# Retention block with a mixture-of-experts layer: router logits as extra columns of the V and output projections, ranking on raw logits

## What is computed

```
x = x + retention(layernorm(x)) @ Wo
x = x + experts(layernorm(x))
```

```
logits = einsum('btd,de->bte', x, Wg)
probs = softmax(logits); top_w, top_i = top_k(probs, 2)
top_w = top_w / (sum(top_w) + 1e-08)
h = square(relu(einsum('td,edh->teh', xt, W1)))
y = einsum('teh,ehd->ted', h, W2)
out = einsum('te,ted->td', combine, y)
```

## Time and profile before

| | |
|---|---|
| median of 3 runs | 290.26 us (289.76 to 290.81) |
| profiled execution, its own time | 288.95 us |
| profiled execution, span | 287.2 us |
| TensorE busy | 274.8 us (96%) |
| weight loads of TensorE | 216.4 us (75%) |
| VectorE busy | 222.4 us (77%) |
| ScalarE busy | 179.3 us (62%) |
| GpSimd busy | 206.1 us (72%) |
| granted TensorE clock, mean | 0.998 |
| 16 DMA engines, main queue | 28.5% of their span |

### The profile page before, as it was taken

How to read it: one execution, slowest core, us unless ns; L and a number is a source line. 1 busy time by engine, 2 the same in 40 slices (tenths; PEclk the granted TensorE clock), 3 DMA queues, 4 the chain that set the end, 5 groups by cost and what they waited for, 6 DMA issues and landing times.

```text
span 287.2 us, 8936 instructions
## 1 busy us (share of the span) xinstructions
PE 274.8 (96%) x3662; PEld 216.4 (75%) x3662; DVE 222.4 (77%) x569; ACT 179.3 (62%) x257; POOL 206.1 (72%) x165
## 2 busy tenths in 40 slices
PE   7999868899999999999999999999999999999995
PEld 5685547678887788777887788777887788878883
DVE  2759758995769875996869965896859768998783
ACT  2345476565782688555974677556875567586861
POOL 2115889879959697769968699569968668566452
PEclk9999999999999999999999999999999999999999
DMA  7329062222250261204440240103420252043101
GB/s 227 120 82 295 5 214 71 86 63 96 70 147 2 78 185 60 89 11 126 128 147 2 79 179 23 59 5 103 157 75 2 77 152 92 19 130 130 75 0 73
DMA packets 13577, 26.80 MB, mean 93 GB/s; under 512 B 1120, under 2 KB 6624, under 8 KB 13536
## 3 DMA queue, kind: packets, MB, share of 16 engines
q1 hardware_dynamic: 13536, 26.23, 28.5%
HBM read 24.00 MB, written 2.23 MB: 91 GB/s over the span
## 4 chain that ended last, share of the span: by engine, by line
PE 52%; POOL 21%; issue 16%; DVE 5%; DMA 2%; ACT 2%; POOLq 1%; DVEq 0%; ACTq 0%
POOL act_lo L1062 17%; PE h_ps L333 7%; PE y_ps L348 6%; PE h_ps L335 6%; PE h_ps L334 5%; PE y_ps L354 5%; PE y_ps L349 5%; PE bank L480 2%; PE bank L492 2%; PE bank L413 2%; POOL x_lo L1032 2%; POOL rstd L1016 1%; PE bank L445 1%; DMA scale<-scratch 1%; PE y_ps L312 1%
## 5 line engine op out<-in xcount | busy, mean ns | idle before, releaser
L1062 POOL TENSOR_TENSOR act_lo<-act_f,act_hi 128x512 fp32r<-128x512 f32 x112 | 145.9, 1325 | 47.7 <-ACT act_f L950 47.6
L760 DVE SCALAR_TENSOR_TENSOR act_s<-h_ps,scale 128x1024 f32<-128x1024 f32 x64 | 77.9, 1217 | 31.1 <-issue 13.6
L945 ACT ACTIVATE act_hi<-act_s 128x1024 fp32r<-128x1024 f32 x64 | 67.9, 1061 | 33.7 <-DVE act_s L760 33.1
L950 ACT ACTIVATE act_f<-act_s 128x1024 f32<-128x1024 f32 x64 | 67.0, 1046 | 0.0
L333 PE MATMUL h_ps<-x_hi,w_lo 128*128 128x512 f32 x128 | 54.1, 422 | 1.0 <-DVE attn L653 1.0
L348 PE MATMUL y_ps<-act_hi,w_lo 128*128 128x512 f32 x128 | 53.9, 421 | 0.0
L335 PE MATMUL h_ps<-x_hi,w_hi 128*128 128x512 f32 x128 | 50.5, 395 | 0.0
L334 PE MATMUL h_ps<-x_lo,w_hi 128*128 128x512 f32 x128 | 50.5, 394 | 0.0
L349 PE MATMUL y_ps<-act_hi,w_hi 128*128 128x512 f32 x128 | 50.3, 393 | 0.0
L354 PE MATMUL y_ps<-act_lo,w_hi 128*128 128x512 f32 x128 | 40.2, 395 | 0.1
L1016 POOL TENSOR_TENSOR rstd<-variance,minus_half 128x4 f32<-128x4 f32 x16 | 17.9, 1119 | 19.1 <-DVE variance L617 18.9
(11 more groups left out here) (121 smaller groups left out, 402.3 us busy)
## 6 DMA issues: line engine op xcount, KB each, us to landing
scale<-scratch SPq DMA_DIRECT2D x32, 512.0 KB, 4.0
x_t_in<-x_tr SPq DMA_DIRECT2D x8, 256.0 KB, 4.8
x_all<-x SPq DMA_DIRECT2D x8, 256.0 KB, 4.6
out<-out_sb SPq DMA_DIRECT2D x8, 256.0 KB, 4.1
scale<-w SPq DMA_DIRECT2D x1, 768.0 KB, 4.8
cst<-constants SPq DMA_DIRECT2D x1, 417.0 KB, 6.0
cst<-constants SPq DMA_DIRECT2D x1, 256.0 KB, 2.8
scale<-w SPq DMA_DIRECT2D x1, 256.0 KB, 6.7
```

The lines of the kernel that those rows point to most:

```text
L760: nc.vector.scalar_tensor_tensor(out=act_s[:, u % 2], in0=h_ps[:, u % 2], scalar=0.0, in1=scale[:, f % 2, e].unsqueeze(1).to_broadcast([P, ...
L945: nc.scalar.activation(act_hi[:, u % 4], act_s[:, u % 2], ACT.Square).then_inc(act_hi_ready, 1)
L950: nc.scalar.activation(act_f[:, u % 2], act_s[:, u % 2], ACT.Square).then_inc(act_f_ready, 1)
L1062: nc.gpsimd.tensor_tensor(act_lo[:, u % 4, n], act_f[:, u % 2, n], act_hi[:, u % 4, n].bitcast(F32), ALU.subtract).then_inc(pool_low_ready, 1)
```

## The change

Router logits are linear in x, so they are gathered where x is made. The table of constants is laid out anew: the centred weight of V carries the 8 router columns beside its 128 (`w_vg`), and the output weight carries `Wo @ Wg` (centred, made once by `route_outputs` and `copy_route`). `project_v` and `project_out` give 136 columns a group; the fourth group goes into another PSUM bank. ScalarE copies the 8 columns of V's result behind x in `x_all` (136 wide now), and `add_attention` adds the rest. `route` and its copy are gone. VectorE ranks the raw logits (`rank_experts`), shifts the ranked ones (`shift_logits`), sums (`weigh`) and marks the two chosen (`mark_chosen`). The root of a share is now the exponential of half the logit (`half_expd`) times the power -1/2 of the denominator (`root_denominators`), which VectorE multiplies in `spread_roots`. The order on every engine is changed with it.

```diff
         def v_place(s, g):
+            if g == GROUPS - 1:
+                return ((y_ps[:], h_bank[3])[s] if s < 2 else bank1[:])[:, 0:WIDE]
+            return ((bank1[:], h_bank[2])[s] if s < 2 else bank2[:])[:, WIDE * g:WIDE * (g + 1)]
...
             def project_v(s):
...
                 elif s >= 2:
                     pe.wait_ge(q_m_ready, s + 1)
                     pe.wait_ge(q_d_ready, s + 1)
+                    pe.wait_ge(x_hi_ready, s)
...
-            def route(s):
...
                 if p < TILES:
                     if n == 0:
                         project_out(p)
                     if n == 2:
                         transpose_x2(p)
-                    if n == 5:
-                        route(p)
...
                     if n == 1:
-                        project_qk(a)
+                        project_k(a)
                     if n == 3:
+                        project_q(a)
+                    if n == 4:
                         transpose_k(a)
-                    if n == 4:
+                    if n == 5:
                         project_v(a)
...
+            def rank_experts(s):
+                raw = x_all[:, s % X_RING, :, P:WIDE]
+                dve.wait_ge(x2_ready, s + 1)
+                for g in range(GROUPS):
+                    last = nc.vector.max(best[:, g], raw[:, g])
+                last.then_inc(rank_step, 1)
...
             def spread_roots(s):
-                dve.wait_ge(root_ready, s + 1)
-                dve.wait_ge(choose_step, CHOOSE_STEPS * (s + 1))
+                dve.wait_ge(r_denom_ready, s + 1)
+                dve.wait_ge(expd_ready, s + 1)
+                nc.vector.tensor_tensor(root[:], half_expd[:], r_denom[:].unsqueeze(2).to_broadcast([P, GROUPS, TOP]),
+                                        ALU.mult).then_inc(spread_step, 1)
...
                 if p < TILES:
                     add_attention(p)
                     statistics(p, 1)
-                if a < TILES:
-                    decay_q(a)
                 scale_h(f, 1)
                 low(u)
+                if p < TILES:
+                    rank_experts(p)
+                    shift_logits(p)
                 if a < TILES:
                     decay_k(a)
+                    decay_q(a)
                 scale_h(f, 2)
                 low(u + 1)
                 if p < TILES:
-                    shift_logits(p)
+                    weigh(p)
+                    mark_chosen(p)
                 scale_h(f, 3)
                 low(u + 2)
                 if p < TILES:
-                    choose(p)
+                    spread_roots(p)
                 if a < TILES:
                     decay_scores(a, decay_order(a)[0:1])
                 scale_h(f, 4)
                 low(u + 3)
                 if a < TILES:
-                    decay_scores(a, decay_order(a)[1:2])
-                if p < TILES:
-                    spread_roots(p)
-                if a < TILES:
-                    decay_scores(a, decay_order(a)[2:])
+                    decay_scores(a, decay_order(a)[1:])
...
                 for g in range(GROUPS):
+                    nc.scalar.copy(x_all[:, s % X_RING, g, P:WIDE], v_place(s, g)[:, P:WIDE])
...
             copy_roots(0)
+            copy_o(1)
+            copy_k(2)
             high_second()
-            copy_o(1)
-            mask_q(2)
-            copy_k(2)
             high_qk()
...
-            def root_shares(s):
-                pool.wait_ge(share_ready, s + 1)
+            def root_denominators(s):
+                pool.wait_ge(denom_ready, s + 1)
                 if s >= 1:
-                    pool.wait_ge(combine_ready, s)
+                    pool.wait_ge(spread_step, SPREAD_STEPS * (s - 1) + 1)
+                nc.gpsimd.tensor_tensor(r_denom[:], denom[:, 2], minus_half[:], ALU.pow).then_inc(r_denom_ready, 1)
```

More of the change, by code:

```diff
@@ L93, in build @@
         minus_half = sb("minus_half", [P, GROUPS])
-        half = sb("half", [P, GROUPS * TOP])
         stats = sb("stats", [P, 2, STAT_RING, GROUPS, 6])
@@ L412, in project_v @@
                 for g in range(GROUPS):
-                    last = pe.matmul(v_bank(s)[:, P * g:P * (g + 1)], x_t_in[:, s % XT_RING, P * g:P * (g + 1)],
-                                     w_center[:, 2], start=True, stop=True)
+                    last = pe.matmul(v_place(s, g), x_t_in[:, s % XT_RING, P * g:P * (g + 1)], w_vg, start=True, stop=True)
                 last.then_inc(v_done, 1)
@@ L498, in project_out @@
                 if s == 0:
-                    pe.wait_ge(second_loaded, DMA)
+                    pe.wait_ge(wog_ready, 1)
                 pe.wait_ge(o_t_ready, s + 1)
                 for g in range(GROUPS):
-                    last = pe.matmul(bank1[:, P * g:P * (g + 1)], o_t[:, s % 2, g], w_out, start=True, stop=True)
+                    last = pe.matmul(out_place(g), o_t[:, s % 2, g], w_out, start=True, stop=True)
                 last.then_inc(wo_done, 1)
@@ L507, in transpose_x2 @@
                 for g in range(GROUPS):
-                    last = pe.transpose(bank1[:, P * g:P * (g + 1)], x_all[:, s % X_RING, g], ident)
+                    last = pe.transpose(bank1[:, P * g:P * (g + 1)], x_all[:, s % X_RING, g, 0:P], ident)
                 last.then_inc(t2_done, 1)
-            def route(s):
-                pe.wait_ge(x_sum_ready, s + 1)
-                if s == 0:
-                    pe.wait_ge(piece_whole, 1)
-                else:
-                    pe.wait_ge(x_hi_ready, s + 1)
-                for g in range(GROUPS):
-                    last = pe.matmul(route_bank(s)[:, EXPERTS * g:EXPERTS * (g + 1)], x_sum[:, s % SUM_RING, P * g:P * (g + 1)],
-                                     wg_whole[:], start=True, stop=True)
-                last.then_inc(router_done, 1)
             def transpose_roots(s):
@@ L607, in statistics @@
                 for g in range(GROUPS):
-                    last = nc.vector.bn_stats(stats[:, which, r, g], xs[:, g])
+                    last = nc.vector.bn_stats(stats[:, which, r, g], xs[:, g, 0:P])
                 last.then_inc(norm_step[which], 1)
@@ L709, in choose, with weigh, weighed @@
+            def weigh(s):
+                def weighed(n):
+                    dve.wait_ge(weigh_step, WEIGH_STEPS * s + n)
                 dve.wait_ge(expd_ready, s + 1)
-                for g in range(GROUPS):
-                    last = nc.vector.max(best[:, g], expd[:, g])
-                last.then_inc(choose_step, 1)
-                nc.vector.tensor_reduce(total[:], expd[:], AX_X, ALU.add).then_inc(choose_step, 1)
-                chosen_step(1)
-                for g in range(GROUPS):
-                    last = nc.vector.max_index(best_at[:, g], best[:, g], expd[:, g])
@@ L734, in choose @@
[L734 to L742 removed]
+                nc.vector.tensor_reduce(total[:], expd[:], AX_X, ALU.add).then_inc(weigh_step, 1)
```

255 lines of the change are left out of this document (136 added, 119 removed).

## The result

The changed kernel takes **333.29 us** (median of 4 runs, 332.0 to 334.87), the kernel before 290.04 us on the same chip (4 runs, 289.76 to 290.81). The ratio is 1.149, with an interval from 1.143 to 1.154: 43 us slower, 13 more than the forecast of 320.0 and just above its range, which ended at 331. In every ratio of this document a run more than 1.5% above the fastest of the same kernel is left out: one of the six of the all-late version and three of the twelve of the tuned version further down, and none elsewhere; medians and spans of values are over all runs.

What follows compares the result with a forecast made beforehand. TensorE's instructions were taken to bound each 32.88 us tile unless an operand comes late. Start +11.0, five tiles +20.0 and last tile -0.85 gave +30 us, carried to the 290.26 median: 320 us, own range 314 to 325, 8-in-10 range 305 to 331.

Steps and rivals of the forecast that it cites:

- The chain of the tile: In each loop tile, late shift, V, y_t, power, root and spread delay unit 5 (expert 5's w1 product) by 4.0 us.
- held and unheld: VectorE's root and spread either last until GpSimd's instruction ends (unit 5 4.0 us late) or run freely (1.8 late).
- The y_t wait: Second product of expert 0 on TensorE stalls 0.8 us for y_t, inside the later stall of unit 5.
- The clock in the tiles: TensorE's clock behind the 3.4 us gap ahead of unit 5: the sum included no cost for a fall.
- a rival at 0.25: Clock falls behind unit 5's gap in every tile, 1.5 to 2.5 us each, five times: +10, 330 us; chance 0.25.
- The start: First tile: later w2 cast delays GpSimd's low parts, the shift, V and unit 5: +11.0 us.
- V's length: First V projection takes 1.75 us instead of 0.86, at 1.2 GHz after a gap of 11 us.
- The last tiles: Tile f=6 has no attention work behind it and only wins its routing slot: -0.85 us.
- five tiles, waits: Tiles f=1 to 5 each lose 4.0 us waiting at unit 5: +20.0 us.
- Lock-free: Root, spread and shift run in GpSimd's gaps: +15, 305.5 us; chance 0.20 with mixtures of it.
- Faster: Every wait stays hidden, so removed routing slots pay: 282.4 us, needing the power to end by 118.4; chance 0.03.

Runs made afterwards that it cites:

- all-late version: Changed kernel, power before act_lo(2), unit 3's scaling before mark_chosen, spread behind all scores, plus start orders, copy_y ahead of copy_v, first-tile exponentials behind copy_v: 294.2 us, ratio 1.014.
- tuned version: all-late version with mark_chosen before shift_logits, q_d before k_d in the loop, a first-tile GpSimd wait for the shift, last-ranking-tile exponentials behind copy_y: 288.48 us, ratio 0.996.
- GpSimd's added wait: Changed kernel with GpSimd, behind the power, waiting until VectorE has made root and spread before act_lo(3): 310.7 us, ratio 1.078.
- the dummies: Changed kernel with twelve dummy products of zeros in the wait ahead of unit 5 of six tiles and 46 in the start: 324.3 us, ratio 1.122.
- sooner cast of w2: Changed kernel with ScalarE's cast of w2 put back ahead of copy_o(1) and copy_k(2) in the start: 328.8 us, ratio 1.138.
- all orders: Changed kernel with power and spread sooner, GpSimd waiting for spread, w2 cast sooner, first-tile k_d and q_d before ranking, copy_y before copy_v: 304.6 us, ratio 1.054.
- kernel before with spread first: Kernel before the change with spread_roots moved ahead of the first block of attention scores on VectorE: 312.6 us, ratio 1.082.
- attn first: Changed kernel with the first attention score block ahead of spread_roots on VectorE in the loop: 323.3 us, ratio 1.119.
- six dummies: Changed kernel with six dummy products of zeros in the wait ahead of unit 5 of six tiles and 22 in the start: 325.6 us, ratio 1.125.
- root sooner: Changed kernel with GpSimd's power ahead of act_lo(2) and VectorE's spread_roots right behind mark_chosen in the loop: 316.8 us, ratio 1.098.

## Why the prediction was right or wrong

**The chain of the tile: right, step by step.** With the frames of the two traces laid on each other at the output projection (160.64 is 102.03, a shift of 58.61), the forecast times and the measured ones are:

| step | forecast | measured |
|---|---|---|
| first part of the shift ends | 110.65 | 110.60 |
| V starts | 112.7 | 112.48 |
| y_t copied from | 115.2 | 114.93 |
| act_lo of unit 2 ends | 120.3 | 120.08 |
| power ends | 121.3 | 121.04 |
| root ends / spread ends | 122.55 / 123.8 | 122.31 / 123.59 |
| unit 5 starts | 124.8 | 124.63 |

The choice between held and unheld (4.0 against 1.8 us) was the largest unknown, and the rows of nearest kind gave the right side. GpSimd's added wait confirms it from the other side. The y_t wait lies inside the chain, as worked out (0.58 us, 0.8 forecast). The Trainium skill (SBUF — State Buffer, "Who interferes with whom") says that a VectorE instruction with two SBUF inputs contends with a GpSimd instruction that reads SBUF. The trace agrees: root, spread, L735 and L738 each end with one of GpSimd's (1.20 to 1.25 us), and so does `chosen` where it was moved later (1.25 and 1.27).

**The clock in the tiles: the step that failed.** The sum put it at nothing and gave it to a rival at 0.25. The rival itself had it right, gap and price: a gap of 3.4 us (measured 3.21) and 1.5 to 2.5 us for a fall (measured some 1.6 us in three of the five tiles and 2.6 in the two whose spell is longer). What the runs showed in place of the sum's nothing is 10.0 us in the five tiles, taken away by the dummies alone, and some 1.6 us more in the first tile. The error is one of reading: the prediction put 3.4 us "between" the gap of 2 us that kept the clock and the end that lost it. But at the end the clock had fallen some 2.1 us behind the last matmul (which ends at 283.94, not at 283.84 as was read):

```profile
283.20 0.74 PE L354 MATMUL y_ps<-act_lo,w_hi 128*128 128x512 f32 x2
```

So 3.4 lies beyond both rows, and the sum should have carried the fall. The sixteen matmuls from which the prediction took the half speed last 0.24 us each, though the column of the clock reads 1.00 there; V at 0.50 here (2.15 us for eight matmuls of 136 columns, 0.27 each) bears the price out all the same. The Trainium skill (TensorE: Matmul & The Clock Gate, "Why this matters for your kernels") advises to leave no long idle gaps between bursts of matmuls, since the clock drops in the middle of a kernel; the six gaps of 3.07 and 3.21 us here agree with it, and the last section shows falls behind shorter ones.

**The start: mechanism right, 2.9 us too small** (+13.9 against +11.0). V came 1.1 us later than worked out, because the copy of k ended 1.4 us later. And the gap at unit 5 of tile f=0 (3.07 us) dropped the clock too, from 68 to 72, which the sum had not taken: from unit 5 on, the tile takes 1.2 us more than before where the sum had 0.4 less, about 1.6 us. The other 0.2 is V's length, 2.15 instead of 1.75. With the orders of the start put right, in the tuned version, tile f=1 begins at 70.09, 0.95 us behind before.

**The last tiles: wrong sign.** The sum had -0.85, since f=6 has no attention behind it; from the last output projection to the end it is 55.06 us against 53.64 before, +1.4. The step forgot that ScalarE's exponentials had moved ahead of the squares of unit 1: they wait for the held shift, `copy_y` waits behind them, and TensorE waits 1.43 us for y_t at 288.09. In the tuned version, with the exponentials behind `copy_y`, that stretch takes 53.0 us, 0.6 less than before: most of the gain that the sum had.

**The account**, spans 331.8 against 287.2, +44.6:

| part | forecast | measured | from |
|---|---|---|---|
| start | +11.0 | +13.9 | 83.04 against 69.14 |
| five tiles, waits | +20.0 | +19.3 | 183.72 (kept warm) against 164.42 |
| five tiles, clock | 0 | +10.0 | 193.70 against 183.72 |
| last tiles | -0.85 | +1.4 | 55.06 against 53.64 |

The clock in the five tiles makes 10.0 of the 14.5 us by which the account exceeds the forecast, and with the first tile some 11.6.

**The rivals.** Lock-free is refuted by the lengths of root and spread. The clock case came true, at 333.3 where it said 330, and the sign that the prediction named for it (a clock below 1 in each tile) is in the trace. "Faster" needed the power to end by 118.4; it ended at 121.0. What the rival had right is that the removed slot is worth something, which the tuned version shows.

## What to carry to other kernels

When an operation with two SBUF operands stands in front of work that another engine waits for, its price is not its own 0.2 us but the rest of the GpSimd instruction that runs beside it; two in a row pay twice. Put such operations where nothing urgent is queued behind them, or let GpSimd wait half a microsecond: a wait added cost less than nothing here. And count what a new wait of TensorE does to its clock: in these runs waits of 1.8 us and more in the tiles cost another 1.5 us behind them, in a part of the tiles or in all.

## What the hardware showed beyond what was expected

The clock falls behind gaps much shorter than 3.2 us, and not always. From the profiled executions, with the granted clock in stretches of 1 us (left out: waits over 5 us, where it fell each time; waits of 1.42 to 1.45 us in the last tiles, where it never did; and waits below 1.6 us in the start, told behind the table):

| wait of TensorE, us | clock fell to 0.50 | where |
|---|---|---|
| 3.07 to 3.22 | 11 of 11 | changed kernel, sooner cast of w2 |
| 2.58, 2.66, 3.37, 4.74 | 4 of 4 | first tile: all late, all orders (two), kernel before with spread first |
| 2.35 | 0 of 1 | first tile, sooner cast of w2 |
| 2.26 | 4 of 5 | kernel before with spread first |
| 2.18 to 2.22 | 5 of 5 | attn first |
| 2.01, 2.04 | 0 of 2 | start of the kernel before; V of the tuned version |
| 1.65 to 1.86 | 4 of 14 | six dummies, root sooner; twelve dummies (start); kernel before with spread first (start and last tiles) |
| 1.57 | 0 of 5 | all orders |
| 1.13 | 0 of 5 | GpSimd waits |

What stands around the wait differs between these rows (state updates of 64x32 behind the 2.2 us, scores or large products behind others), so the lengths alone do not order them; which of it decides was not tried. In the start it fell behind shorter waits too: behind 1.2 to 1.5 us ahead of tile 1's state updates in four of eight runs (once 1.51, three times 1.23 or 1.24), behind 1.06 us ahead of the first product with w1 in one of seven, and inside tile 1's output projection, where 0.76 us is followed after one matmul by 0.93 to 1.24 us, in three of six; behind the other waits of 0.9 to 1.3 us there it stayed up. So no wait of the table is so short that the clock was safe behind it everywhere.

A fall behind the same wait costs 1.5 to 1.6 us in the three pairs of tiles above, whether the wait was 1.8 or 2.3 us; in two tiles of the changed kernel (f=2 and f=5) the low clock lasted nearly 7 us instead of 3 to 4, and the tile took 39.3 and 39.4 us instead of 38.3 or 38.4.

Not only operations with two SBUF tensors were held. The shift (a tensor_scalar of 128x8 that reads one SBUF tensor and two columns of scalars) was held in every tile of the changed kernel (in the five tiles 1.77 or 1.78 us for its four instructions, the first of them 1.20 us, up to x_lo's end; in the tuned version, where it starts behind x_lo, the four take 0.86), and in the run with all orders late the four shifts of the first tile took 3.84 us together, behind a power, x_lo and an act_lo that GpSimd issued without a pause.
